# Causal mask of a transformer's second layer: GpSimd zeroes the probabilities instead of a mask matmul under the scores

## The reference

```python
q, k, v = (to_heads(q), to_heads(k), to_heads(v))     # 16 heads of 8 features
q = q * cos + _rotate_half(q) * sin
k = k * cos + _rotate_half(k) * sin
att = jnp.einsum('bhtd,bhsd->bhts', q, k) * scale
causal = jnp.tril(jnp.ones((T, T), dtype=bool))
att = jnp.where(causal, att, jnp.finfo(att.dtype).min)
att = jax.nn.softmax(att, axis=-1)
y = jnp.einsum('bhts,bhsd->bhtd', att, v)
```

## Time and profile before

| | us |
|---|---|
| median of 3 runs | 1470.41 |
| lowest, highest | 1470.06, 1474.22 |
| the profiled execution | 1472.95, its span 1471.2 |

### The profile page before, as it was taken

One profiled execution on the slowest core, in us unless ns is written; L12 is line 12 of the kernel. 1 busy time (PEld: TensorE's weight loads), 2 busy tenths in 40 slices (PEclk: granted clock), 3 DMA queues, 4 the chain that ended last, 5 costly groups with the idle time before them and its releaser, 6 DMA issues. The chain is left out here.

```text
span 1471.2 us, 36081 instructions
## 1 busy us (share of the span) xinstructions
PE 1124.8 (76%) x11411; PEld 782.7 (53%) x11411; DVE 1085.5 (74%) x2949; ACT 843.2 (57%) x1844; POOL 553.4 (38%) x572
## 2 busy tenths in 40 slices
PE   2599999999999996128999999999999957203220
PEld 1366666666666653016777777777777734102120
DVE  1479999999999976515676777767777756898996
ACT  1267777777777663615666666666666635203554
POOL 5323323333233303364444554445544232002555
PEclk9899999999999998558999999999999988655555
DMA  5545554545545413044444544444444302000111
GB/s 144 140 115 119 119 132 111 131 111 127 125 115 133 100 34 118 14 100 102 109 114 109 116 110 112 108 113 115 107 116 101 81 16 93 7 0 1 30 36 50
DMA packets 115921, 137.26 MB, mean 93 GB/s; under 512 B 12112, under 2 KB 101520, under 8 KB 106640
## 3 DMA queue, kind: packets, MB, share of 16 engines
q1 hardware_dynamic: 112704, 132.25, 37.1%
q10 hardware_dynamic: 3152, 4.20, 1.1%
HBM read 85.03 MB, written 37.75 MB: 83 GB/s over the span
## 5 line engine op out<-in xcount | busy, mean ns | idle before, releaser
L353 DVE TENSOR_REDUCE attn_negmax<-attn_row_ps 128x2 f32<-128x512 f32 (+1 forms) x1024 | 607.0, 618 | 238.7 <-PE attn_row_ps L535 226.3
L297 ACT ACTIVATE attn_probs<-attn_col_ps 128x512 f32<-128x512 f32 (+1 forms) x1024 | 540.3, 547 | 243.3 <-PE attn_col_ps L557 226.7
L535 PE MATMUL attn_row_ps<-attn_k_st,attn_q_st 72*128 72x256 bf16 (+1 forms) x2048 | 369.9, 262 | 16.9 <-DMA attn_k_st<-attn_scratch 15.2
L557 PE MATMUL attn_col_ps<-attn_q_st,attn_k_st 74*128 74x256 bf16 (+1 forms) x2048 | 370.6, 262 | 2.4 <-ACT attn_probs L297 1.0
L574 PE MATMUL attn_out_ps<-attn_probs,attn_v_sb 128*32 128x256 f32 (+1 forms) x4096 | 250.0, 362 | 1.3 <-ACT attn_probs L297 1.3
L557 PEld LDWEIGHTS attn_col_ps<-attn_q_st,attn_k_st 74*128 74x128 bf16 x2048 | 180.2, 99 | 92.6 <-ACT attn_probs L297 31.6
L535 PEld LDWEIGHTS attn_row_ps<-attn_k_st,attn_q_st 72*128 72x128 bf16 x2048 | 202.0, 99 | 42.8 <-issue 16.6
L282 POOL TENSOR_TENSOR attn_rstd<-attn_var,minus_half 128x2 f32<-128x2 f32 x64 | 45.5, 711 | 386.4 <-DVE attn_var L418 386.4
L531 PE MATMUL attn_row_ps<-mask_qk,ident_h 128*128 128x256 bf16 x512 | 141.0, 276 | 24.4 <-DMA attn_k_st<-attn_scratch 23.9
L574 PEld LDWEIGHTS attn_out_ps<-attn_probs,attn_v_sb 128*32 128x32 f32 x4096 | 107.4, 109 | 87.4 <-issue 22.5
L553 PE MATMUL attn_col_ps<-mask_kq,ident_h 128*128 128x256 bf16 x512 | 141.8, 277 | 14.6 <-DMA attn_q_st<-attn_mT_sb 11.9
(11 more groups left out here) (229 smaller groups left out, 1682.1 us busy)
## 6 DMA issues: line engine op xcount, KB each, us to landing
attn_q_st<-attn_scratch SPq DMA_DIRECT2D x192, 192.0 KB
attn_k_st<-attn_scratch SPq DMA_DIRECT2D x192, 192.0 KB
attn_scratch<-attn_parts SPq DMA_DIRECT2D x64, 384.0 KB, 3.0
attn_scratch<-attn_parts SPq DMA_DIRECT2D x64, 128.0 KB, 3.1
attn_x_in<-in_L_attn_x_dram SPq DMA_DIRECT2D x32, 128.0 KB, 2.2
moe_xs<-x_all SPq DMA_DIRECT2D x8, 512.0 KB, 3.1
attn_x_in<-x_mid SPq DMA_DIRECT2D x32, 128.0 KB, 2.1
ffn_xs<-x_mid SPq DMA_DIRECT2D x16, 256.0 KB, 2.3
```

What stands on the lines that cost most here:

```text
L297: nc.scalar.activation(probs[:, u % 2, j, 0:W], col_ps[:, n % 2, 0:W], ACT.Exp, scale=scale).then_inc(probs_kept, 1)
L353: nc.vector.tensor_reduce(negmax[:, t, 2 * p:2 * p + 2], row_ps[:, row_bank(st, u), 0:2 * keys].rearrange("p (a k) -> p a k", a=2), AX_X, ...
L535: last = nc.tensor.matmul(bank[:, a * keys:(a + 1) * keys], q_st[0:KROWS, sl, h, t * P:(t + 1) * P], k_st[0:KROWS, sl, h, 0:keys], start=n ...
L557: last = nc.tensor.matmul(bank[:, t * N:(t + 1) * N - first], k_st[0:rows, sl, h, t * P:(t + 1) * P], q_st[0:rows, sl, h, first:N], start= ...
```

## The change

The mask matmul under the column scores goes, and with it the constant `mask_kq`. The column scores of both layers are now plain matmuls. In the second layer GpSimd sets the entries above the diagonal to 0 behind the exponentials, in one `affine_select` for each unit of four heads (`keep_seen`), and PV waits for that. PV's places move in the second layer from n = 6, 10, 14 and 2 (next round) to n = 8, 12, 0 and 4 (next round), `transpose_o` from 4 to 7, ScalarE's copy of its input from 2 to 5 and VectorE's normalisation from 3 to 6. `probs` gets a third buffer in both layers. The first layer's places stay.

```diff
-      "attn1": dict(act_xT=0, act_mT1=0, act_qk=1, act_oT=2, act_onT=10, act_mT0=11,
-                    dve_o=3, dve_split0=9, dve_v=5, dve_y=12, dve_var=14, dve_ln=15,
-                    pe_xT=0, pe_mT1=1, pe_pv3=2, pe_qk=1, pe_oT=4, pe_pv=6, pe_v=3, pe_onT=10, pe_mT0=11, pe_y=12)}
+      "attn1": dict(act_xT=0, act_mT1=0, act_qk=1, act_oT=5, act_onT=10, act_mT0=11,
+                    dve_o=6, dve_split0=9, dve_v=5, dve_y=12, dve_var=14, dve_ln=15,
+                    pe_xT=0, pe_mT1=1, pe_qk=1, pe_oT=7, pe_v=3, pe_onT=10, pe_mT0=11, pe_y=12,
+                    pe_pv={0: (4, 2), 4: (4, 3), 8: (3, 0), 12: (3, 1)})}
+PROBS = 3
...
+            def keep_seen(st, lag, u):
+                pool.wait_ge(probs_kept, st.seq(lag, H, 4 * u + 4))
+                apart(pool, mem)
+                diagonal = probs_of(st, lag, u).rearrange("p j (t q) -> p j t q", t=TB)[:, :, :, 0:P]
+                nc.gpsimd.affine_select(out=diagonal, in_=diagonal, compare_op=ALU.is_ge, fill=0.0, base=0,
+                                        pattern=[[0, 4], [0, TB], [1, P]], channel_multiplier=-1)\
+                    .then_inc(seen_kept, 1)
...
+                if st.has(4) and causal:
+                    keep_seen(st, 4, 3)
                 if st.has(0):
...
                         pool.wait_ge(turned, st.seq(0, c=1))
+                if st.has(3) and causal:
+                    keep_seen(st, 3, 0)
+                if st.has(0):
...
                     nc.gpsimd.tensor_tensor(rest[:, :, :], qk[:, :, :], parts[:, :, 0, :], ALU.subtract)\
                         .then_inc(rest_kept, 1)
+                if st.has(3) and causal:
+                    keep_seen(st, 3, 1)
+                if st.has(0):
...
                     nc.gpsimd.tensor_tensor(parts[:, :, 2, :], rest[:, :, :], parts[:, :, 1, :], ALU.subtract)\
                         .then_inc(lo_kept, 1)
+                if st.has(3) and causal:
+                    keep_seen(st, 3, 2)
...
-                            wait(act, pv_ready, st.seq(3, 4, u - 1))
-                        nc.scalar.activation(probs[:, u % 2, j, 0:W], col_ps[:, n % 2, 0:W], ACT.Exp,
+                            wait(act, pv_ready, st.seq(3, 4, u + 1 - PROBS))
+                        nc.scalar.activation(probs_of(st, 3, u)[:, j, 0:W], col_ps[:, n % 2, 0:W], ACT.Exp,
...
-                if causal:
-                    seen = bank[:, 0:2 * N].rearrange("p (a q) -> p a q", a=2)
-                    nc.tensor.matmul(seen[:, :, 0:P], ident_h[:, :], mask_kq[:, :, :],
-                                     start=True, stop=False, skip_group_check=True)
...
-                pe.wait_ge(probs_kept, st.seq(lag, H, 4 * u + 4))
+                if causal:
+                    pe.wait_ge(seen_kept, st.seq(lag, 4, u + 1))
+                else:
+                    pe.wait_ge(probs_kept, st.seq(lag, H, 4 * u + 4))
```

More of the change, by code:

```diff
@@ L102, in attention @@
     x_all, wqk, wv, wo, bqk, bv, bo = (mem[k] for k in ("x_all", "wqk", "wv", "wo", "bqk", "bv", "bo"))
-    ident, ident_h, mask_qk, mask_kq = (mem[k] for k in ("ident", "ident_h", "mask_qk", "mask_kq"))
+    ident, ident_h, mask_qk = (mem[k] for k in ("ident", "ident_h", "mask_qk"))
     scale = float(D) ** -0.5
@@ L166, in attention @@
         v_cleared, k_ones = sem("v_cleared"), sem("k_ones")
+        seen_kept = sem("seen_kept")
         block = ctx.enter_context(nc.Block())
@@ L174, in attention, with probs_of @@
         UNITS, ROW_BANKS = NH * TB, 3
+        def probs_of(st, lag, u):
+            return probs[:, (4 * (st.off - lag) + u) % PROBS, :, :]
         def row_bank(st, u):
@@ L558, in score_cols @@
                                             k_st[0:rows, sl, h, t * P:(t + 1) * P], q_st[0:rows, sl, h, first:N],
-                                            start=not causal, stop=True, skip_group_check=causal)
+                                            start=True, stop=True)
                 last.then_inc(cols_ready, 1)
@@ L575, in sum_values @@
                                                 v_sb[:, st.slot(lag), t, 32 * h:32 * h + 32],
-                                                probs[:, u % 2, j, t * N:(t + 1) * N - first],
+                                                probs_of(st, lag, u)[:, j, t * N:(t + 1) * N - first],
                                                 start=a == 0 and t == 0, stop=a == 1 and t == TB - 1,
@@ L590, in step @@
                         transpose_max(st, 3, 1)
-                    if n == at["pe_pv3"] and st.has(4):
-                        sum_values(st, 4, 3)
+                    if n in at["pe_pv"] and at["pe_pv"][n][0] == 4 and st.has(4):
+                        sum_values(st, *at["pe_pv"][n])
                     if n == at["pe_qk"] and st.has(0):
@@ L596, in step @@
                         transpose_o(st)
-                    if n in (at["pe_pv"], at["pe_pv"] + 4, at["pe_pv"] + 8) and st.has(3):
-                        sum_values(st, 3, (n - at["pe_pv"]) // 4)
+                    if n in at["pe_pv"] and at["pe_pv"][n][0] == 3 and st.has(3):
+                        sum_values(st, *at["pe_pv"][n])
                     if n == at["pe_v"] and st.has(2):
@@ L1660, in _ @@
         def _(pool):
-            for t in (mem["ident"], mem["ident_h"], mem["mask_qk"], mem["mask_kq"]):
+            for t in (mem["ident"], mem["ident_h"], mem["mask_qk"]):
                 nc.gpsimd.memset(t[:], 0.0).then_inc(zeroed, 1)
@@ L1673, in _ @@
                                     base=0, pattern=[[0, 2], [-1, P]], channel_multiplier=1).then_inc(consts, 1)
-            nc.gpsimd.affine_select(out=mem["mask_kq"][:], in_=mem["mask_kq"][:], compare_op=ALU.is_ge, fill=MASKED,
-                                    base=0, pattern=[[0, 2], [1, P]], channel_multiplier=-1).then_inc(consts, 1)
             nc.gpsimd.affine_select(out=diagonal[:, :], in_=diagonal[:, :], compare_op=ALU.is_ge, fill=0.0,
@@ L1725, in _ @@
             last.then_inc(lora_ready, 1)
-            pe.wait_ge(consts, 6)
+            pe.wait_ge(consts, 5)
             for s, of in enumerate((0, 2)):
```

11 lines of the change are left out of this document (6 added, 5 removed).

## The result

The changed kernel takes 1557.65 us (median of 4 runs, 1553.94 to 1561.63) against 1470.24 us for the kernel before on the same chip: ratio 1.0593, 95% interval 1.0566 to 1.062. The profiled execution's span is 1557.4 us; before it was 1471.2.

What follows compares the result with a forecast made beforehand. The second layer was taken as bound by a recurrence through GpSimd, 16.64 us a round; +3.06 us over 29 rounds (+88.7) and the rounds after the last store made +85, 1556 us, and clock falls +32, 1588 us; range 1542 to 1636.

Steps and rivals of the forecast that it cites:

- the sign: Whole kernel: the change makes it slower, chance 0.94, against 0.04 faster and 0.02 the same.
- the likeliest case: Second layer: the round grows and TensorE's clock falls in about three rounds of four; 1588 us, chance 0.45.
- the first rival: Second layer: the round grows but TensorE's clock holds; 1556 us, chance 0.36.
- The ring: Second layer's round: closed chain through TensorE, ScalarE, GpSimd, SyncE's store and maxima's transfer to next column scores, 16.59 us.
- Rivals 3 and 4: Second layer: TensorE's stream is the bound, 1416 us, chance 0.04; the change does nothing measurable, chance 0.02.
- Masks: Mask matmuls out: 0.11 us each, only two of a round's 16 ahead of the QK projection, -0.22 us a round.
- PV ahead of the projection: Unit 2's PV moves to head 0, ahead of the QK projection: +0.88 us a round.
- The selects: GpSimd, between rotation and last part: two selects of 1.2 us each ahead of the store, +2.4 us a round.
- New waits: PV waits for selects: TensorE stops 1.3 us at head 8, last scores through at 16.9 us, costing nothing of itself.
- The clock: TensorE in the second layer: falls to half speed in about three rounds of four, 1.5 us each, +32 us.
- The tail: Rounds after the last store: some 48 masks less, -4.8 us, and a late last select, +1.3 us.
- the stop at the round's end: TensorE at the end of every second-layer round: waits 2.8 us, 19.7 less 16.9.

Runs made afterwards that it cites:

- e2: Kernel before with the maxima's transfer issued ahead of the two stores on SyncE's queue: 1451.18 us, ratio 0.9884.
- e1: Kernel before with only the mask matmul taken out, causal part of the column scores left out: 1476.29 us, ratio 1.0069.
- e3: Kernel before with two selects on an unread tile, behind GpSimd's rotation and behind its first subtraction: 1550.49 us, ratio 1.0559.
- e5: Changed kernel without its four selects a round and PV's wait for them, causal part left out: 1493.91 us, ratio 1.0177 to the kernel before.
- e9: Kernel before without the mask matmul (causal part left out) and with the maxima's transfer ahead of the stores: 1411.24 us, ratio 0.9596.
- e6: Changed kernel with PV of unit 2 at head 2, behind the QK projection, instead of head 0: 1552.32 us, ratio 1.0562 to the kernel before.
- e8: e7 with unit 0's select ahead of the rotation, PV of unit 3 at head 2, transposes of o at head 5: 1549.17 us.
- e7: Changed kernel with the maxima's transfer ahead of the two stores on SyncE's queue: 1530.8 us, ratio 1.0433 to the kernel before.
- e4: Kernel before with one select on an unread tile at the round's start, where GpSimd is idle: 1476.22 us, ratio 1.0054.
- e11: e7 with selects of units 1 and 2 behind the last part, PV at heads 10, 14, 2 and 5, transposes of o at 8: 1477.93 us.
- e12: e11 with unit 3's select waiting until VectorE has split the maxima, and PV of unit 1 at head 15 instead of 14: 1441.51 us.

## Why the prediction was right or wrong

The time lies in the range (1542 to 1636), the sign and the mechanism held, and the likeliest case did not: 1557.65 us measured, 1588 forecast, 1556 in the first rival. That the time is so near the rival's is luck: the rival had the selects 16 us too dear, no falls of the clock and a tail 10 us too short, and these cancel. Step by step:

- **The ring.** Right. It was predicted as the sum of the earlier trace rows and is shown by e2: opening it takes 16 us off the kernel before (1467.58 on that chip to 1451.18). Rivals 3 and 4 are out by e1, e3 and e5.
- **Masks.** Right in the ring's terms: rounds at full clock lose 0.2 us (e1), and 1.16 of TensorE's 1.7 us come out once the ring is open (e9 against e2).
- **PV ahead of the projection.** +0.88 a round predicted; the stretch to the projection's end grew from 2.78 to 3.48, +0.70, which with 0.22 of masks taken off is 0.92.
- **The selects.** 1.2 us each was 1.10 measured (mean 1099 ns, in 128 of them), and in the ring they added 0.93 each (8.25 to 10.11 for two), because they fill the 0.2 us hand-overs between GpSimd's dependent steps. I had named that for the lower bound and not taken it. This term was 0.54 us a round too large, 16 us in all. The Trainium skill (GPSIMD Engine Reference, section 3.1) gives 1.03 cycles an element for small bodies and 1.8 at best for larger ones. For 1024 elements at 1.2 GHz these are estimates of 0.88 and 1.5 us, without a fixed part: the measured 1.10 is nearer to the first, and the second did not come. The slope that the prediction read from the earlier trace rows, 1 ns an element, is 1.2 cycles, so it fitted the first only roughly.
- **New waits.** The stop at head 8 was put at 1.3 us; 1.15 measured. The list of waits after, 740 to 1200 us:

```profile
PE attn_col_ps L578 <- DMA attn_q_st<-attn_mT_sb: 29.8, 24, 1.5
...
PE attn_out_ps L598 <- POOL attn_probs L254: 26.2, 23, 1.1
...
PE attn_in_ps L526 <- ACT attn_qk L349: 24.2, 24, 1.1
...
PE attn_in_ps L496 <- DVE attn_mparts L391: 21.8, 24, 0.9
```

The last of these was missing in the prediction: VectorE blocked by GpSimd, 0.9 us a round at head 11. The stop at the V projection stood in my layout (5.4 us) but was not counted as a stop. The four stops of a round, 1.22 + 1.15 + 1.05 + 0.91, and e9's 14.94 make 19.27; the rounds at full clock are 19.25. TensorE's end of the round was thus a microsecond later than laid out, and the ring half a microsecond shorter: its last stop was 1.2 us, not 2.8.
- **The clock.** The step that failed, for that reason. I put a stop of 2.8 us into the argument and took falls in three rounds of four, +32 us. Measured was a granted clock under 1.00 in six of 29 rounds; five of them were 0.9 to 2.8 us longer than those at full clock, some 10 us together. Two of the five are the first and third of the 29, and the kernel before has a slow first one too (18.73 us at 0.73), so between the two kernels the falls make some 8 us. Three stretches around one of them, columns as in the earlier trace rows:

```profile
1066.70:1070.10 3.40, 2.49 (x32) 1.59 (x30) 2.49 (x5) 1.52 (x4) 3.32 (x4) 1.00 0.00 0
1070.10:1073.50 3.40, 2.10 (x23) 1.59 (x21) 3.00 (x11) 1.54 (x4) 0.93 (x3) 1.00 0.67 195
1073.50:1080.30 6.80, 6.80 (x39) 3.76 (x37) 2.94 (x6) 3.09 (x8) 0.95 (x1) 0.51 0.21 54
```

2.49 of 3.4 us busy was followed by full clock, 2.10 of 3.4 was followed by half. In the kernel before 2.08 kept it, so these rows don't tell a stretch before a fall from one before none, and I had read too much out of them. That falls can come with stops well under 3 us and land on the ring was right: the clock was under 1.00 in 10 of 29 rounds of e1, in 20 of e3, in 20 of e6 and in all of e8. Spread over those rounds they cost 1.6 us each in e1, 1.7 in e3 and 1.0 in e6, where the prediction took 1.5.
- **The tail.** -3.5 us predicted, +6.5 measured after the last store. The round without stores went from 14.0 to 13.4 (transfer at 1230.22 to 1243.61), so the masks did come out there. The next one went from 15.0 to 16.4: the granted clock was 0.76 in 1249 to 1253 and 0.81 in 1253 to 1257, and 0.83 in all of 1249 to 1280, where the kernel before had 1.00 in the same part of its layer (1169 to 1200). That these falls make the whole difference was not tested.

In the sum: selects -16, clock -22, tail +10, start of the layer -3 us against the forecast of 1588; these make 1557. The step that failed is thus the stop at the round's end, put at 2.8 us where 1.2 came, and with it the falls, put at three rounds of four where six of 29 had them; the ring, the price of the PV unit and the sign held.

## What to carry to other kernels

In a software pipeline add up one round's chain of hand-overs across engines and queues before believing a busy share: where the sum was the round, here, work off the chain was worth nothing (e1) and work on it counted, on an engine that was half idle too (e3), less what it filled of pauses. A small transfer behind a store in an in-order queue can close such a chain; reordering two DMA issues made the kernel 1.2% faster here, where the mask's removal alone made it 0.7% slower. And work moved to GpSimd has a second price: VectorE's small casts and subtractions on SBUF waited here until the GpSimd instruction beside them was over, so give the critical ones a gap. A stretch's busy share says little about the clock that it will get (e7 against e1 below); look at it in the trace after each change.

## What the runs showed of the hardware

- A VectorE cast of 16 elements took 0.16 to 0.18 us alone and 0.62 to 1.11 us where it began behind the start of a GpSimd instruction, ending with it (e3, e4, e5, e11, e12); the subtraction of 16 elements behind it took up to 1.09. In the kernel before the cast began when GpSimd's instruction had 0.11 us left (947.88 in L270, over at 947.99), and the subtraction fell into the pause of 0.19 us behind that.
- Removing TensorE work inside a round of fixed length lowered the granted clock, 1.00 to 0.96 in 900 to 1100 us, and made the kernel 0.7% slower (e1). The busy share alone doesn't tell: e1 was busy 180.37 of 200 us, and e7, busy 160.04 of 200 with its stops spread over the round, kept 1.00. What exactly makes the clock fall stays open.
- From issue of the maxima's transfer on SyncE's queue to the first matmul that waited for it: 2.35 to 2.41 us, before and after.
- A select of 1024 fp32 elements per partition took 1.09 to 1.11 us on GpSimd, all 128 of the changed kernel.
